# Cross-attention with exponentials, masks, v units and context turns in other places, and the third layer norm's root on GpSimd

## The reference, cut to what matters

```
x = x + self_attention(layernorm(x))                     # 16 heads of 64, causal
x = x + cross_attention(layernorm(x), ctx, mask)         # 16 heads of 32, 750 keys
x = x + experts(layernorm(x), router_w, wg, wu, wd)      # 8 experts, the best 2 per token

cross-attention:  q = x @ Wq;  k = ctx @ Wk;  v = ctx @ Wv
                  scores = q k^T / sqrt(32), masked keys at -max
                  out = softmax(scores) @ v;  return out @ Wo
layernorm:        (x - mean) / sqrt(var + 1e-5)
router:           logits = layernorm(x) @ router_w.T
```

## Time and profile before

| | |
|---|---|
| Time, median of 3 runs | 3887.45 us (3887.23 to 3889.75) |
| Profiled execution's own time | 3881.1 us |
| Its span | 3879.0 us |
| Mean granted clock of TensorE | 0.978 of full |
| Busy share of the span | TensorE 95%, VectorE 62%, ScalarE 45%, GpSimd 32% |
| Largest group on VectorE | L1580, the maximum, 512 operations of 936 ns |
| Largest group on ScalarE | L1414, the exponential, 768 of 542 ns |
| Values (L1160) | first at 1140.3 us, last at 2504.3 us |

### The profile page before, as it was taken

One profiled execution on the slowest core, in us unless ns is written; L12 is line 12 of the kernel. 1 busy time (PEld: TensorE's weight loads), 2 busy tenths in 40 slices (PEclk: granted clock), 3 DMA queues, 4 the chain that ended last, 5 costly groups with the idle time before them and its releaser, 6 DMA issues. The chain is left out here.

```text
span 3879.0 us, 84806 instructions
## 1 busy us (share of the span) xinstructions
PE 3671.3 (95%) x28086; PEld 3160.2 (81%) x28086; DVE 2415.3 (62%) x5666; ACT 1733.0 (45%) x4277; POOL 1256.8 (32%) x1189
## 2 busy tenths in 40 slices
PE   7999999999979999999999999849999999999998
PEld 6888888888767887877778887639999899899997
DVE  6888888888746777666667776575434434434343
ACT  4554545555535555555555555313333333333332
POOL 1333333333325555555555555410101101011010
PEclk9999999999989999999999999869999999999999
DMA  4222222222333434343343443223424324334232
GB/s 123 58 53 63 57 58 58 57 58 63 95 104 94 104 104 108 102 114 101 100 106 99 104 105 89 67 67 86 118 81 117 108 85 117 86 113 113 80 103 64
DMA packets 315521, 347.58 MB, mean 90 GB/s; under 512 B 45247, under 2 KB 231975, under 8 KB 315396
## 3 DMA queue, kind: packets, MB, share of 16 engines
q1 hardware_dynamic: 305796, 318.25, 30.4%
q0 software_dynamic: 9600, 27.58, 2.5%
HBM read 181.62 MB, written 38.65 MB: 57 GB/s over the span
## 5 line engine op out<-in xcount | busy, mean ns | idle before, releaser
L1580 DVE TENSOR_REDUCE x_mx<-x_psS 112x1 f32<-112x752 f32 x512 | 479.4, 936 | 423.0 <-PE x_psS L1135 417.9
L2318 DVE TENSOR_TENSOR hid<-e_psU,act_g 128x280 f32<-128x280 f32 x256 | 115.2, 450 | 679.2 <-PE e_psU L34 679.1
L1414 ACT ACTIVATE x_pt<-x_psE 125x448 f32<-125x448 f32 x768 | 389.5, 542 | 277.1 <-PE x_psE L1147 271.0
L1028 POOL TENSOR_TENSOR part<-x_pt 125x448 f32<-125x448 f32 x255 | 291.8, 1144 | 626.1 <-ACT x_pt L1414 626.0
L1964 POOL DMA_INDIRECT out<-ex_y,sidx x40 | 38.0, 951 | 1045.7 <-DVE ex_y L2351 1038.4
L612 POOL TENSOR_TENSOR qks<-qks,cos 128x448 f32<-128x448 f32 x128 | 147.8, 1155 | 676.1 <-DMA qks<-qk 676.1
L1135 PE MATMUL x_psS<-k_st,q_st 97*112 97x376 f32 x1024 | 289.8, 364 | 39.4 <-DVE x_mx L1580 25.8
L2109 ACT ACTIVATE act_g<-e_psG 128x280 f32<-128x280 f32 x256 | 103.7, 405 | 471.2 <-PE e_psG L34 470.5
L32 PE MATMUL pj<-xT_hi,win_hi 128*128 128x224 f32 x1024 | 302.8, 296 | 1.4 <-DVE xT_lo L652 1.3
L32 PE MATMUL e_psG<-ex_hi,g_hi 128*128 128x280 f32 x1024 | 303.0, 296 | 0.9 <-issue 0.9
L33 PE MATMUL e_psU<-ex_lo,u_hi 128*128 128x280 f32 x1024 | 297.3, 290 | 3.2 <-issue 3.2
(11 more groups left out here) (287 smaller groups left out, 10746.1 us busy)
## 6 DMA issues: line engine op xcount, KB each, us to landing
k_st<-kT SPq DMA_DIRECT2D x768, 93.8 KB, 2.2
raw_g<-in_L_ffn_wg SPq DMA_DIRECT2D x128, 256.0 KB, 3.3
raw_u<-in_L_ffn_wu SPq DMA_DIRECT2D x128, 256.0 KB, 3.5
raw_d<-in_L_ffn_wd SPq DMA_DIRECT2D x128, 256.0 KB, 2.7
qks<-qk SPq DMA_DIRECT2D x512, 56.0 KB, 2.0
q_st<-qT SPq DMA_DIRECT2D x384, 56.0 KB, 2.0
ctxt<-in_ctx SPq DMA_DIRECT2D x16, 1125.0 KB
xt<-in_x SPq DMA_DIRECT2D x16, 448.0 KB, 3.7
```

The lines of the kernel that those rows point to most:

```text
L1028: pool.tensor_tensor(part[:], pt[j][:, 0, :], pt[j][:, 1, :], ALU.add).then_inc(parted, 1)
L1414: act.activation(pt[j][:, i, :], psE[(j + i) % 2][0:KR, 0:2 * T], ACT.Exp, scale=XD ** -0.5).then_inc(exp_done, 1)
L1580: dve.tensor_reduce(mx[:, j, h:h + 1], psS[0:HT, :, 0:376], AX.XY, ALU.max).then_inc(s_taken, 1)
L2318: dve.tensor_tensor(h[i][:, halves[s]], psU[:, 0:CH], act_g[i][:, halves[s]], ALU.mult).then_inc(S["mul"], 1)
```

## The change

1. `exps`: in j3 all three exponentials are taken ahead of the first gap; in j0 to j2 the third stays between the gaps.
2. `mask` steps 1 and 2 both move to g1's second gap of j3.
3. C21 (the turn on TensorE, its upper part on ScalarE, its lower on VectorE) moves from g2 to the second gap of g3's j0; K00 waits for C20 and K01 for C21 instead of for C10 and C11.
4. V01 moves to g3's second gap of j1, V02 to the first gap of j2, V03 to the second gap of j2. The second gap of j3 is left empty in g3. `UNITS` follows.
5. The three Newton steps and the shift go to GpSimd: `root(b - 2, j)` behind the block sum of j = 0, 1, 2 in g0, 14 operations per batch instead of 10, each waited for by the next. `normalise` waits for the new semaphore `newton`. The last two batches' roots stay on VectorE behind the loop. GpSimd's loop is now `all_batches`, 16 head sums per pass (8 before).
6. Two semaphores of the first stage go (`q_filled`, whose place `xres_ready` takes, and `w_lo`, for which nothing waits).

```diff
-         "K30 M1_2 O1 K31 V14 V15 C00 C10 Q0 C20 M0_2 C01 Q1 C11 C21 "
-         "K00 V00 M1_3 K01 V01 V02 M0_3 V03").split()
+         "K30 M1_2 O1 K31 V14 V15 C00 C10 Q0 C20 M0_2 C01 Q1 C11 "
+         "K00 C21 V00 M1_3 K01 V01 V02 V03 M0_3").split()
...
-RLN_STEPS = 2 + 2 + 3 + 9 + 1
+RLN_STEPS = 2 + 2 + 3
+NEWTON_STEPS = 3 * 4 + 2
...
+                    def root(b, i):
+                        k = NEWTON_STEPS * b
+                        a, y, w, shift = (lnw[:, 2 * i:2 * i + 2] for i in range(4))
+                        if i == 0:
+                            hold(pool, gate, rln, RLN_STEPS * b + RLN_STEPS)
+                        pool.tensor_tensor(a, y, y, ALU.mult).then_inc(newton, 1)
+                        pool.wait_ge(newton, k + 4 * i + 1)
+                        pool.tensor_tensor(a, a, w, ALU.mult).then_inc(newton, 1)
+                        hold(pool, gate, newton, k + 4 * i + 2)
+                        pool.tensor_scalar(a, a, -0.5, 1.5, ALU.mult, ALU.add).then_inc(newton, 1)
+                        pool.wait_ge(newton, k + 4 * i + 3)
+                        pool.tensor_tensor(y, a, y, ALU.mult).then_inc(newton, 1)
+                        hold(pool, gate, newton, k + 4 * i + 4)
+                        if i == 2:
+                            pool.tensor_scalar(shift, mv[:, :, 0], -1.0, None, ALU.mult).then_inc(newton, 1)
+                            pool.wait_ge(newton, k + 13)
+                            pool.tensor_tensor(shift, shift, y, ALU.mult).then_inc(newton, 1)
+                            pool.wait_ge(newton, k + 14)
+                    def body(b, first, last):
+                        for g in range(4):
+                            for j in range(0 if first and g == 0 else 4):
+                                sum_blocks(4 * b + g - 1, (g + 3) % 4, [j])
+                                if g == 0 and j < 3 and not below(b, 2):
+                                    root(b - 2, j)
+                    all_batches(pool, body)
+                    sum_blocks(4 * B - 1, 3, range(3))
...  TensorE
-                                project_k(U(f"K{ng}{j}"), ng, j, *([U(f"C1{j}")] if g == 3 else []))
+                                project_k(U(f"K{ng}{j}"), ng, j, *([U("C21" if j else "C20")] if g == 3 else []))
...  ScalarE
-                        act.wait_ge(rln, RLN_STEPS * b + RLN_STEPS)
+                        if isinstance(b, int) and b == B - 1:
+                            act.wait_ge(rln, RLN_STEPS * B + 20)
+                        else:
+                            act.wait_ge(newton, NEWTON_STEPS * b + NEWTON_STEPS)
...
-                                if g == 2 and not last:
-                                    mask(b + 1, 1)
...
-                                    if not last:
-                                        mask(b + 1, 2)
...
                                 elif g == 1:
+                                    if not last:
+                                        mask(b + 1, 1)
+                                        mask(b + 1, 2)
...
-                                    exps(n - 1, j, (0, 1))
+                                    exps(n - 1, j, range(3) if j == 3 else (0, 1))
                                 first_gap(g, j)
-                                if prev:
+                                if prev and j < 3:
                                     exps(n - 1, j, (2,))
...  VectorE
-                                if g == 0 and old:
-                                    router_norm(b - 2, 3)
...
-                                if g == 0 and old:
-                                    router_norm(b - 2, 5)
...
-                                if g == 0 and old:
-                                    router_norm(b - 2, 4)
-                                elif g == 3 and not first:
+                                if g == 3 and not last:
+                                    low_ctx(b, 2, 1)
+                                if g == 3 and not first:
                                     router_norm(b - 1, 0, [U(f"O{h}") for h in range(2)])
```

More of the change, by code:

```diff
@@ L632, in _ @@
                     pool.wait_ge(v_full, 4 * B)
-                    pool.memset(op.q_st[96:99, :, :].bitcast(F32), 1.0).then_inc(op.q_filled, 1)
-                    pool.wait_ge(op.q_filled, 1)
+                    pool.memset(op.q_st[96:99, :, :].bitcast(F32), 1.0).then_inc(xres_ready, 1)
+                    pool.wait_ge(xres_ready, B + 1)
                 @block.vector
@@ L1035, in sum_blocks @@
                             pool.wait_ge(pt_summed, n + 1)
-                    for t in range(2):
-                        sum_blocks(t, t)
-                    with pool.Fori(1, 2 * B - 1) as q:
-                        sum_blocks(2 * q, 0)
-                        sum_blocks(2 * q + 1, 1)
-                    sum_blocks(4 * B - 2, 0)
-                    sum_blocks(4 * B - 1, 1, range(3))
+                    def root(b, i):
[24 more added lines that the diff above has]
+                    sum_blocks(4 * B - 1, 3, range(3))
                 @block.tensor
@@ L1213, in first_gap @@
                                 elif g == 3 and not last:
-                                    project_v(U("V01"), 0, 1)
+                                    project_v(U("V02"), 0, 2)
                             elif j == 3:
@@ L1231, in second_gap @@
                                 elif g == 3 and not last:
+                                    turn_ctx(U("C21"), b + 1, 2, 1)
                                     project_v(U("V00"), 0, 0)
@@ L1246, in second_gap @@
                                     project_v(U("V15"), 1, 5)
+                                elif not last:
+                                    project_v(U("V01"), 0, 1)
                             elif j == 2:
@@ L1257, in second_gap @@
                                 elif g == 3 and not last:
-                                    project_v(U("V02"), 0, 2)
+                                    project_v(U("V03"), 0, 3)
                             else:
@@ L1269, in second_gap @@
                                     turn_ctx(U("C11"), b + 1, 1, 1)
-                                    turn_ctx(U("C21"), b + 1, 2, 1)
-                                elif g == 3 and not last:
-                                    project_v(U("V03"), 0, 3)
                         for g in range(4):
@@ L1454, in first_gap @@
                                 elif g == 3 and not last:
-                                    out_v(U("V01"), 0, 1)
+                                    out_v(U("V02"), 0, 2)
                             elif j == 3:
@@ L1472, in second_gap @@
                                 elif g == 3 and not last:
+                                    high_ctx(U("C21"), 2, 1)
                                     out_v(U("V00"), 0, 0)
@@ L1487, in second_gap @@
                                     out_v(U("V15"), 1, 5)
-                                    if not last:
-                                        mask(b + 1, 2)
+                                elif not last:
+                                    out_v(U("V01"), 0, 1)
                             elif j == 2:
@@ L1500, in second_gap @@
                                 elif g == 3 and not last:
-                                    out_v(U("V02"), 0, 2)
+                                    out_v(U("V03"), 0, 3)
                             else:
@@ L1513, in second_gap @@
                                     high_ctx(U("C11"), 1, 1)
-                                    high_ctx(U("C21"), 2, 1)
-                                elif g == 3 and not last:
-                                    out_v(U("V03"), 0, 3)
                         for g in range(4):
@@ L1606, in router_norm @@
                     def router_norm(b, part, units=None):
-                        k = RLN_STEPS * b
+                        k = RLN_STEPS * b + (10 if isinstance(b, int) and b == B - 1 else 0)
                         a, y, w, shift = (lnw[:, 2 * i:2 * i + 2] for i in range(4))
@@ L1660, in first_gap @@
                             if j == 0:
-                                if g == 0 and old:
-                                    router_norm(b - 2, 3)
-                                elif g == 1 and not last:
+                                if g == 1 and not last:
                                     low_x(b, 1)
@@ L1666, in first_gap @@
                                     residual(U("O0"), b - 1, 0)
-                                elif g == 3 and not last:
-                                    low_ctx(b, 2, 1)
                             elif j == 1:
@@ L1732, in _, with root @@
                     all_batches(dve, body)
+                    def root(n):
+                        a, y, w, shift = (lnw[:, 2 * i:2 * i + 2] for i in range(4))
+                        for i in range(3):
+                            dve.wait_ge(rln, n + 3 * i)
+                            dve.tensor_tensor(a, y, y, ALU.mult).then_inc(rln, 1)
```

(14 more changed lines are left out.)

17 lines of the change are left out of this document (3 added, 14 removed).

## The result

| | before | after | forecast |
|---|---|---|---|
| median of the timed runs, us | 3887.34 (4 runs) | 3841.34 (4 runs, 3833.68 to 3842.39) | 3829 (3812 to 3868) |
| ratio to before, 95% interval | | 0.9878 [0.9866, 0.9891] | 0.985 |
| profiled execution (its span), us | 3881.1 (3879.0) | 3833.7 (3831.9) | 3823 |
| cross-attention and router in the profile, from the first scores to the sorting of the routing weights (`wsort`), us | 1430.7 | 1378.7 | about 1373 |

The change makes the kernel 1.2% faster, inside the range. 47.4 us went in the profiled execution where 58 was forecast. The second measurement of the same kernel, further down, gave 3831.4 and a ratio of 0.9877: the ratio is the steadier figure.

The account below looks back on a forecast made before the run. TensorE, busy 1214.9 of 1280 us, was the bound, so only its idle time could be won; 14.8 + 14.3 - 1.5 + 11.7 - 1 + 7.8 + 11.1 = 57.2, plus about 1, took 3887.45 to 3829 us (3812 to 3868).

Parts of the forecast that it names:

- 1 Newton steps off VectorE: In g0, TensorE's scores no longer wait for the maximum: 1.06 us a batch, 14.8 us over 14 batches.
- 3 third exponential: End of g0: values no longer wait for j3's third exponential: 0.95 us a batch, 14.3 us over 15 batches.
- 4 masks: In g2, TensorE's third unit no longer waits for the exponential of j2: net 0.78 us a batch, 11.7 us.
- 5 C21: Moving C21 saves 1.10 us in g2 and costs 0.58 in g3: net 0.52 us a batch, 7.8 us.
- 6 v units: In g3, V01 fills the gap holding only the totals: net 0.74 us a batch, 11.1 us.
- the steps: Signs in TensorE's waits: for exponential near zero (values, units), transposes' under 5 us, for maximum under 6, none in g0 j2.
- One sign: In g0, GpSimd's two-column rows at 0.2 us, with ScalarE's normalisation not waiting for them.
- C: Rival: waits are only rearranged, Newton and exponential gains stay, half is handed on; about 3875 to 3890 us, chance 0.05.
- A: Rival: stalls handed on through thin margins, 19 to 31 us return, 3848 to 3860; 0.23 shared with moderately slow GpSimd steps.
- booked for margins: Delay from the earlier third exponential where little slack is left behind the maxima: 0.1 us a batch, 1.5 us in all.
- Part 2: Root steps on GpSimd in g0, 14 small operations a batch: cost nothing, covered by GpSimd's idle time and ScalarE's 1.4 us slack.
- x: Time of one small GpSimd root operation with its gap: 0.27 us taken, bounds 0.08 to 0.75, lateness starting at 0.39.

Follow-up runs that it names:

- e1: Changed kernel with the Newton steps back on VectorE at their old places in g0: 1.06 us a batch longer in g3>g0, g0>g1 0.07 shorter.
- e2: Changed kernel with the third exponential of j3 back behind the first gap: 0.81 us longer in g3>g0 and 0.54 in g2>g3, 1.35 in all.
- e3: Changed kernel with mask steps 1 and 2 back from g1 to g2: 0.79 us a batch longer in g1>g2.
- e4: Changed kernel with C21, its turn and both copies back at the end of g2: 1.55 us more in g1>g2, 0.73 less in g2>g3, 0.82 net.
- e5: Changed kernel with V01, V02 and V03 each one place later, as before: 0.56 us a batch longer in g2>g3.
- e11: Changed kernel with both the third exponential of j3 and V01, V02, V03 at their old places: g2>g3 is 19.07 us, 0.58 more.
- after_again: The changed kernel measured once more, unchanged: median 3831.4 us, ratio 0.9877, expert stage 1264.2 us.
- e6: Changed kernel with 14 more unused two-column GpSimd products that the normalisation waits for: g0>g1 27.72 us, 4.95 more; ratio 1.0046 to the kernel before.

## Why the prediction was right, and its gain too large

| per batch, us | forecast | single undo |
|---|---|---|
| 1 Newton steps off VectorE | 1.06 | 1.06 (e1) |
| 3 third exponential | 0.95, less 0.1 | 0.81 in g3>g0, 0.54 in g2>g3 (e2) |
| 4 masks | 0.78 | 0.79 (e3) |
| 5 C21 | 0.52 (1.10 - 0.58) | 0.82 (1.55 - 0.73) (e4) |
| 6 v units | 0.74 | 0.56 (e5) |
| sum | 4.05, less 0.1 | 4.58 |
| shared by two edits | none | 0.52 (e11) and 0.60 (g1>g2) |
| g0>g1 longer (DMA, below) | none | 0.12 (in no undo's term) |
| all together | 3.95 | 3.40 (87.16 to 83.76, medians) |

The undos close to within 0.06 us: 4.58 less 0.52, 0.60 and 0.12 is 3.34, against 3.40 by the period's medians and 3.38 by the four blocks'. The first overlap is 0.54 and 0.56 less the 0.58 of both together. The second, 0.60, is e3's 0.79 and e4's 1.55, which add to 2.34, against the 1.74 by which g1>g2 fell; e2 leaves this block alone. That what C21 and the exponential do to each other makes it rests on e4's timeline and was not tested; that the masks and C21 share it isn't ruled out, since those two were not undone together.

The bound was right: TensorE's idle time was what could be won, and the waits of the earlier trace rows fell to about what the steps said. One sign failed: ScalarE's normalisation does wait for the roots. Undoing an edit brings its wait back, so C is out. A is out as a case: nothing was handed on to VectorE in g0 and g1, where the maxima kept pace (scores 2.41 us behind the values' start, as forecast), and GpSimd did not end late.

**Parts 1 and 4** came to within 0.01 us (part 1's own figures, 0.96 and 0.09, add to 1.05). They are the two where the released instruction goes on as in an undisturbed place, and where what lies behind it was followed to the next wait.

**The term that was mis-sized: what TensorE does right behind the stall** (parts 3, 5 and 6). The prediction put the next start at a spacing read elsewhere. By block, in us per batch:

| block | forecast | measured | what shows the difference |
|---|---|---|---|
| g1>g2 | -1.88 (0.78 + 1.10) | -1.74 | values 0.42 behind C11, where 0.27 was put |
| g2>g3 | -0.16 (0.58 - 0.74) | +0.13 | M1_3 2.08 behind the scores (1.42 before), 0.66 where 0.58 was put; V01's gap, below |
| g3>g0 | -2.01 (1.06 + 0.95) | -1.89 | values 0.51 behind the transposes of x, where 0.31 + 0.02 was put |
| g0>g1 | 0 | +0.12 | the DMA waits, below |
| booked for margins | +0.1 | | nothing of the kind in g0 and g1 |

The sum is 3.95 forecast and 3.38 measured. In g3>g0 and g1>g2 the exponential and the banks were there in time (no wait stands there); values behind transposes start 0.42 to 0.51 us behind them in these rows, scores or units 0.31 to 0.38, and I had used the latter spacing. In g2>g3 V01 does not fit into its gap without lengthening it. TensorE after:

```profile
1585.17 0.51 PE L1158 MATMUL x_psS<-k_st,q_st 97*112 97x376 f32 x2
...
1587.25 0.57 PE L1148 MATMUL x_pj<-ident,x_mx 112*128 112x112 f32 x4 [0.18 <-DVE kT L1599]
...
1590.66 0.59 PE L1195 MATMUL x_psYZ<-ptsum,x_ones 125*32 125x224 f32 x8
1592.35 0.51 PE L1158 MATMUL x_psS<-k_st,q_st 97*112 97x376 f32 x2
...
1598.61 2.48 PE L1183 MATMUL x_psYZ<-x_pt,x_v 125*32 125x224 f32 x48
```

The scores start 1.69 us behind the totals, 1.11 in the earlier trace rows: V01 lengthens that gap by 0.58. From these scores to the values it is 6.26 us (1592.35 to 1598.61), 7.41 before (1608.79 to 1616.20), so the end of g3 is 1.15 shorter without V03. Part 6 is worth 0.57, as e5 measured (0.56), not 0.74.

**The account of the stage.** Periods 3 to 13 gained 0.57 us less each than forecast, 6.3 us together. Period 2 gained 1.71 instead of 3.95, 2.2 less, for a DMA (below). The first two and the last two batches, for which the sum had left 58 - 12 x 3.95 = 10.6, gained 13.1, 2.5 more. So 6.3 + 2.2 - 2.5 = 6.0, which is 58 less 52.0. The other 4.6 us of the profiled execution's 10.6 are the expert stage, 5.2 longer in that execution, less 0.6 elsewhere. At least 3.0 of the 5.2 are not the change's doing, since the same kernel took 1264.2 in after_again, and with 32 nops 1261.7, no more than before; of the kernel before there is one trace only. The second measurement's median, 3831.4, lies 10 us below the first; against the kernel before of its own set it is the same 1.2%. The two profiled executions differ by 1 us only (3833.7 and 3832.7), so no trace tells where the 10 us lie.

**Part 2** cost nothing, as forecast, by less than thought. The step is 0.195 us (42 of L1044: 195/195/197 ns), but with the gaps 14 of them take 5.0 us of GpSimd's time in a batch, x = 0.36, not 0.27, and the point where lateness begins was put at 0.39. ScalarE waits:

```profile
ACT x_xr L1421 <- POOL x_lnw L1055: 11.5, 14, 0.9
```

It ends its first exponential of g1 at 1537.54; TensorE asks for it at 1538.03: 0.5 us is left of the 1.4. The forecast extrapolated the duration well and the gaps badly: 0.08 between long sums is not the gap between short operations that wait for each other. The Trainium skill, "GPSIMD Engine Reference", section 3.1, gives the 1.96x for 2048 columns; carried over to two columns it gave the estimate of 0.31 per operation. Measured is 0.195 against VectorE's 0.16 at its shortest, a ratio of 1.2, so for two columns that ratio overstates.

**Unforeseen** was a wait of the scores for a DMA (`k_st<-mk`): two waits of 2.0 us in all, 1.73 of it in g0>g1 of period 2. Shorter delays lie in the same place: g0>g1 takes up to 23.02 us in single batches of the steady part, where it was 22.65 throughout before. The prediction had looked at the k rows that leave behind K01's lower part. The late ones are others, those of K10 and K11, which the scores of g1 need. SyncE issues the next batch's context and mask right ahead of them. Here are the mask's load before, then (period 2, after) the mask's load, the third and the fourth transfer of k's rows, and the scores that wait:

```profile
1535.05 4.13 SPq L919 DMA_DIRECT2D mk<-in_mask_BxS_bf  x1
...
1353.66 3.92 SPq L920 DMA_DIRECT2D mk<-in_mask_BxS_bf  x1
1359.36 0.59 SPq L955 DMA_DIRECT2D k_st<-kT  x1
1360.00 0.85 SPq L957 DMA_DIRECT2D k_st<-mk  x1
1368.13 0.60 PE L1158 MATMUL x_psS<-k_st,q_st 97*112 97x376 f32 x2 [1.73 <-DMA k_st<-mk]
```

From issue to landing the mask takes 13.2 us and the third transfer 7.4, so both land at 1366.8; the fourth takes 8.0 and lands at 1368.0. In batches 1 to 14, before and after, the third lands within 0.35 us of the mask; in batch 15, which has no such loads, it takes 2.1 us. Before, the mask is issued 14.1 us ahead of the values of g0 and the fourth transfer lands 3.0 us before the scores of g1. After, with g3 and g0 shorter, it is 11.7 us and 0.13 (both medians), and in no trace do scores start less than 0.11 behind the landing: the change has used up the transfers' cover. The single undos agree. With e1, e2, e5 and e11, which lengthen g2>g3 or g3>g0, the mask is issued 12.2 to 13.1 us ahead and there is next to no such wait (0.15 us at most); with e3 and e4, which lengthen g1>g2, it is 11.7 and the waits are there (2.0 and 2.2 us in period 2). What holds the third transfer back, the context's load or the mask's, no run tells, and the order of issue was not changed. Until it is, further time won between K01 and g1 would go into this wait.

## What to carry to other kernels

Undo the edits one by one and also in pairs where they touch the same block: here the single undos added to 4.58 us a batch and the whole gave 3.40. 0.52 of the difference is an early exponential and a moved unit that each covered for the other. When a stall is to go, price the next start by a row in which the same two kinds of instruction follow each other without a wait, not by the spacing of another pair. Work moved to a side engine is free up to its cover and then costs more than its length: 14 small operations cost nothing, 28 made the kernel slower than before. A transfer for which nobody waits has a margin too: measure it from landing to use, and take off what each edit shortens the way in between. Here 3.0 us became 0.1.

## What the runs showed of the hardware

- Small GpSimd operations of two columns take 0.195 us, 0.268 start to start in e6's chain of 14 in which each waits for the one before, and 0.36 on average with the gaps around groups of four to six.
- A stall of 3.1 us on TensorE cost 4.95: the granted clock was 0.61 in the 4 us behind it and 1.00 ahead of the stall (e6).
- A short transfer can land with a longer one that was issued before it: 7.4 us from issue to landing for one of k's rows behind the context and mask loads, 2.1 us for the same transfer in the batch without them.
- A VectorE operation of two columns can last until the GpSimd sum beside it ends, with one input as well as with two. In the earlier trace rows it was the form with two; here two integer operations with one input each, on VectorE, and the GpSimd sum beside them. The first starts in the gap before the sum and takes 0.17 us, the second ends with the sum, in each of the 15 batches in which a sum runs beside it (0.56 to 0.61 us; 0.17 in the one without):

```profile
1600.94 0.17 DVE L1650 TENSOR_SCALAR x_lnw<-x_lnw 112x2 int32<-112x2 int32 x1
1601.02 0.67 POOL L1035 TENSOR_TENSOR ptsum<-part 125x224 f32<-125x224 f32 x1
1601.14 0.56 DVE L1652 TENSOR_SCALAR x_lnw<-x_lnw 112x2 int32<-112x2 int32 x1
```

  The Trainium skill, "GPSIMD Engine Reference", section 8, names the shared SBUF interfaces, and contention with VectorE operations that have two SBUF inputs or run in a 2-port mode. The rows with two inputs agree; whether the form with one input ran in such a mode no row tells. GpSimd's own sums are not slowed (255 of L1029 take 1.127 to 1.162 us).
